# Two layers of graph attention on one core: every engine's steps in another order within the turn, some of them across its border

## What is computed

```python
# layer 0: 6 heads of 64, masked dot-product attention
q, k, v = heads(x @ Wq + bq), heads(x @ Wk + bk), heads(x @ Wv + bv)
probs = softmax(q @ k.T / 8 + where(adj, 0, -9e15))
x = layernorm(x + (probs @ v) @ Wf + bf)
# layer 1: 12 heads of 32, additive attention with a gate
h = x @ W                                  # per head
attn = leaky(tanh(h) @ w_src + (tanh(h) @ w_dst).T, 0.2)
attn = softmax(where(adj, attn, -999))
feat = elu(attn @ h + b)
gate = sigmoid(x @ H_w.T + H_b)
x = layernorm(x + gate * feat + (1 - gate) * x)
```

## Time and profile before

| | |
|---|---|
| median of three runs | 1347.98 us |
| the profiled execution's own time | 1350.65 us |
| its span, from the first to the last instruction | 1348.9 us |
| mean granted clock of TensorE | 0.98 of full speed |
| busy: PE, DVE, POOL, ACT | 1200.5, 1077.4, 1006.0, 990.9 us |
| mean load of the DMA queues | 33 GB/s |
| PE's share of the chain that ended last | 53% |

### The profile page before, as it was taken

How to read it: one execution, slowest core, us unless ns; L and a number is a source line. 1 busy time by engine, 2 the same in 40 slices (tenths; PEclk the granted TensorE clock), 3 DMA queues, 4 the chain that set the end, 5 groups by cost and what they waited for, 6 DMA issues and landing times.

```text
span 1348.9 us, 37937 instructions
## 1 busy us (share of the span) xinstructions
PE 1200.5 (89%) x13193; PEld 1066.4 (79%) x13193; DVE 1077.4 (80%) x2138; ACT 990.9 (73%) x2058; POOL 1006.0 (75%) x941
## 2 busy tenths in 40 slices
PE   4899999999999999999999999999999999999963
PEld 4788788888878888878888887888887888887752
DVE  5478788888888888888888888888888888888864
ACT  4377777777777777777777777777778778777753
POOL 1257877778887777887777788777788777878766
PEclk9799999999999999999999999999999999999976
DMA  3100010111010111101011100011110101110000
GB/s 130 50 27 28 16 39 25 37 37 37 14 37 24 37 37 38 37 14 37 24 37 37 37 19 33 25 36 37 37 37 14 37 24 37 37 37 26 15 13 24
DMA packets 46172, 44.86 MB, mean 33 GB/s; under 512 B 24757, under 2 KB 41146, under 8 KB 46138
## 3 DMA queue, kind: packets, MB, share of 16 engines
q1 hardware_dynamic: 46138, 44.42, 10.1%
HBM read 31.22 MB, written 12.58 MB: 32 GB/s over the span
## 4 chain that ended last, share of the span: by engine, by line
PE 53%; POOL 13%; issue 12%; DVE 10%; ACT 9%; DMA 1%; SPq 0%; DVEq 0%; POOLq 0%; ACTq 0%
PE lin L427 31%; PE tp L600 5%; DVE z L1084 4%; ACT p L785 3%; POOL f L1306 3%; PE zp L528 2%; POOL y L1331 2%; PE tp L565 2%; POOL v_res L1274 2%; PE zp L586 2%; PE fp L612 2%; POOL v_part L1278 2%; PE fp L553 2%; PE zp L590 2%; POOL rstd L1295 1%
## 5 line engine op out<-in xcount | busy, mean ns | idle before, releaser
L1300 POOL TENSOR_TENSOR z<-z,z_max 128x1536 f32<-128x1536 f32 x64 | 176.3, 2755 | 18.0 <-DVE z_max L1091 18.0
L1291 POOL TENSOR_TENSOR rstd<-rstd,half_neg 128x1 f32<-128x1 f32 x64 | 35.2, 549 | 163.3 <-DVE rstd L1071 163.3
L1253 POOL TENSOR_TENSOR prod<-th,w_sd_rows 128x768 f32<-128x768 f32 x64 | 120.1, 1876 | 36.0 <-ACT th L716 36.0
L824 ACT ACTIVATE p1t_hi<-tp 128x512 f16<-128x512 f32 x192 | 110.6, 593 | 37.6 <-PE tp L600 37.6
L1099 DVE SCALAR_TENSOR_TENSOR p1t_lo<-tp,p1t_hi 128x512 f16<-128x512 f32 x192 | 129.4, 688 | 8.0 <-ACT p1t_hi L824 5.0
L612 PE MATMUL fp<-h_part,p1t_hi 128*128 128x33 bf16 x2304 | 115.6, 179 | 4.5 <-DVE p1t_lo L1099 4.4
L612 PEld LDWEIGHTS fp<-h_part,p1t_hi 128*128 128x128 f16 x2304 | 102.5, 97 | 18.4 <-issue 12.7
L600 PE MATMUL tp<-ident,z 128*128 128x128 f32 x768 | 109.5, 280 | 7.4 <-ACT z L819 5.9
L1084 DVE SCALAR_TENSOR_TENSOR z<-zp,z 128x1536 f32<-128x1536 f32 x64 | 111.8, 1748 | 3.2 <-ACT z L794 3.2
L1091 DVE TENSOR_REDUCE z_max<-z 128x12 f32<-128x1536 f32 x64 | 111.3, 1738 | 0.1
L785 ACT ACTIVATE p<-zp,p_shift 128x128 f32<-128x128 f32 x384 | 105.6, 382 | 5.9 <-DVE p_shift L1022 5.9
(11 more groups left out here) (163 smaller groups left out, 4805.3 us busy)
## 6 DMA issues: line engine op xcount, KB each, us to landing
xt_raw<-x_t SPq DMA_DIRECT2D x32, 384.0 KB, 3.6
x_raw<-x SPq DMA_DIRECT2D x32, 384.0 KB, 3.1
out<-out_tile SPq DMA_DIRECT2D x64, 192.0 KB, 1.9
dst_row<-sd_t SPq DMA_DIRECT2D x192, 3.0 KB
adj<-adj SPq DMA_DIRECT2D x64, 32.0 KB, 1.9
z<-Wq SPq DMA_DIRECT2D x1, 576.0 KB, 3.6
z<-Wk SPq DMA_DIRECT2D x1, 576.0 KB, 4.6
p<-Wv SPq DMA_DIRECT2D x1, 576.0 KB, 6.6
```

The costliest lines, as they stand in the source:

```text
L824: act.activation(p1t_hi[:, g, 4 * N * k:4 * N * (k + 1)], tp_bank(f"wt{g}{k}")[:, :], ACT.Copy, scale=PSCALE).then_inc(wt_hi[k][g].sem, 1)
L1253: pool.tensor_tensor(prod[:, g, :].rearrange("p (s d) -> p s d", s=2), th[:, g:g + 1, :].to_broadcast([128, 2, D]), rows["w_sd"][:, :].rea ...
L1300: pool.tensor_tensor(zs, zs, z_max[:, g, :].unsqueeze(2).to_broadcast([128, H1, N]), ALU.subtract)\
```

## The change

The same steps, each engine's in another order; no step is added or removed, and no step itself is touched. Some calls change from `late` to `step` or back, which moves them across the border of a turn. The lists of PSUM users follow:

```diff
-TP_USERS = ("ct1", "wt00", "wt01", "wt02", "x1t0", "wt10", "x1t1", "wt11", "wt12", "pt01", "sdt", "pt00",
-             "pt11", "pt10", "ct0")
+TP_USERS = ("ct0", "ct1", "wt00", "wt01", "wt02", "x1t0", "wt10", "x1t1", "wt11", "wt12", "pt01", "pt00", "sdt", "pt10", "pt11")
-LATE_USERS = ("g1", "z1", "ct1", "pr0", "pr1")
+LATE_USERS = ("ct0", "g1", "z1", "ct1", "pr0", "pr1")
...
+                turn.late(0, context_transposes, 0)
                 turn.late(1, gate_rows, 1)
                 turn.late(1, attention1, 1)
...
-                turn.step(0, context_transposes, 0)
                 turn.step(0, attend0, 1)
...
-                turn.late(1, z_copy, 1)
...
+                turn.step(1, z_copy, 0)
+                turn.step(1, keep_x1, 0)
+                turn.step(0, context_high, 0)
...
+                turn.step(1, z_leak, 0)
+                turn.step(0, context_inverse, 1)
```

More of the change, by code:

```diff
@@ L405, in store @@
                     sp.dma_start(out_d[turn.pair(2), :, g, :], out_tile[:, g, :]).then_inc(stored[g].sem, 16)
-                turn.late(0, load_adj1)
+                turn.late(-1, load_adj0)
                 turn.late(-1, load_x)
+                turn.late(2, store, 0)
+                turn.step(0, load_adj1)
+                turn.step(1, targets_flat)
                 turn.step(-1, load_transposed_x)
-                turn.step(1, targets_flat)
-                turn.step(-1, load_adj0)
-                turn.late(2, store, 0)
                 turn.late(2, store, 1)
@@ L635, in body @@
                 turn.step(2, attend1, 0, 2)
+                turn.step(2, weights1_transposes, 1, 0)
                 turn.step(1, hidden, 0)
-                turn.step(2, weights1_transposes, 1, 0)
                 turn.step(1, x1_transposes, 1)
@@ L1143, in shift_norm1 @@
                         .then_inc(norm1_shift[g].sem, 1)
-                turn.late(0, context_inverse, 1)
-                turn.late(2, variance1, 0)
                 turn.late(0, context_norm, 1)
-                turn.late(1, z_leak, 0)
                 turn.late(0, context_low, 0)
@@ L1331, in mix @@
                     pool.tensor_tensor(y2[:, g, :], f[:, g, :], x1_kept[:, g, :], ALU.add).then_inc(y2_ready[g].sem, 1)
-                turn.late(2, gated_features, 1)
-                turn.late(2, mix, 1)
                 turn.late(-1, next_x_low)
                 turn.late(1, z_subtract, 0)
-                turn.late(1, hidden_part3, 0)
+                turn.late(2, mix, 1)
+                turn.late(1, hidden_part3, 1)
+                turn.step(1, mask1_bias)
                 turn.late(0, deviation0, 0)
                 turn.late(1, z_subtract, 1)
-                turn.late(1, hidden_part3, 1)
                 turn.late(0, deviation0, 1)
-                turn.late(2, deviation1, 0)
                 turn.step(0, value_residue, 0)
@@ L1346, in body @@
                 turn.step(2, features_negative, 0)
+                turn.late(2, deviation1, 0)
                 turn.step(1, source_target_products, 0)
@@ L1349, in body @@
                 turn.step(2, features_difference, 0)
-                turn.step(1, mask1_bias)
+                turn.step(0, value_part3, 0)
+                turn.step(1, hidden_residue, 0)
                 turn.step(2, gated_features, 0)
+                turn.step(0, value_residue, 1)
                 turn.step(2, mix, 0)
-                turn.step(0, value_residue, 1)
-                turn.step(0, value_part3, 0)
                 turn.step(2, features_bias, 1)
                 turn.step(2, features_negative, 1)
+                turn.step(0, value_part3, 1)
                 turn.late(2, deviation1, 1)
-                turn.step(0, value_part3, 1)
-                turn.step(1, hidden_residue, 0)
+                turn.step(1, hidden_residue, 1)
                 turn.step(2, features_difference, 1)
-                turn.step(1, hidden_residue, 1)
+                turn.step(2, gated_features, 1)
+                turn.step(1, hidden_part3, 0)
             turns(pool, passed, body, biases_loaded)
```

87 lines of the change are left out of this document (43 added, 44 removed).

## The result

| | before | after |
|---|---|---|
| median, beside each other on one chip | 1348.32 us (1346.89 to 1348.87) | 1388.49 us (1387.32 to 1389.52) |
| ratio, 95% interval | | 1.0299 [1.0282, 1.0317] |
| span of the profiled execution | 1348.9 us | 1385.6 us |
| mean granted clock of TensorE | 0.98 | 0.946 |

1312 us was forecast; the slower rival was put at 1361 us, and by another mechanism. The turn first, in the timeline of SP of the changed kernel (start and duration in us): the six DMAs of the flat rows, turn by turn.

The account below looks back on a forecast made before the run. The prediction took TensorE's work with holes in the turn's last third as the bound; −1.9 + 0.5 + 0.2 = −1.2 us over 30 turns gave 1312 us. The range was 1278 to 1336 us.

Parts of the forecast that it names:

- the slower rival: The targets' chain comes later because `scores_shift(0)` loses the port: +0.45 us a turn, 1361 us, chance 0.10.
- What bounds the kernel: TensorE's work with holes in the turn's last third; reordering could win some 3 us a turn.
- the two holes: TensorE's stops before `context_transposes(0)`, 1.35 us, and before `attention1(1)`, 0.76 us, laid to steps queued on DVE and ACT.
- Term 1, the end of the turn: `attention1(0)` to the next `attention1(1)`: 3.35 to 3.65 us in place of 5.43, −1.9 us a turn.
- Term 2, the targets' chain: DVE's small steps wait for GpSimd, `source_target_transposes` comes 0.8 us later: +0.5 us a turn.
- the rule in the prediction: On DVE, a step with all inputs in SBUF stands still while a GpSimd step runs; PSUM readers do not.
- Term 3, SP: On SP, the later load of transposed x delays `z_subtract(0)` and TensorE: +0.2 us a turn, 0 to +0.45.
- Term 4: Everything else in the turn keeps its distance from its neighbours within 0.3 us: nothing.
- Parts 2 and 3 don't wait: In the targets' chain they run free of GpSimd: −2.2 us a turn, 1282 us, chance 0.22.
- The gain goes to DMA: On SP, flat rows and transposed x land later: −0.4 us a turn, 1336 us, chance 0.15.
- `scores_shift(0)` loses the port: On DVE it waits for GpSimd's second product, delaying the targets' chain: +0.45 us a turn, 1361 us, chance 0.10.

Follow-up runs that it names:

- Experiment 2: The changed kernel with part 1, residue, part 2 and part 3 as one instruction each over both graphs instead of two: 1313.78 us.
- experiment 3: The kernel before with only `value_part3(0)` and `hidden_residue(0)` moved on GpSimd, right behind `features_difference(0)`: 1387.09 us.
- experiment 1: The changed kernel with GpSimd's `value_part3(0)` and `hidden_residue(0)` back behind `mix(0)`: 1319.62 us.
- experiment 6: The changed kernel with ten unused 512-column matmuls on TensorE ahead of its wait for the targets' chain: 1364.88 us.
- experiment 7: The changed kernel with SP's list as it was before the change: 1382.12 us.
- experiment 8: The changed kernel, chain steps merged, two GpSimd steps behind `mix(0)`: 1307.67 us; then SP's old list: 1300.56; then fewer flat-row DMAs: 1300.44; then `weights0_low(0, 0)` earlier: 1300.37.
- experiment 5: The changed kernel, two variants: GpSimd waits for the targets' chain before `value_part3(0)`, 1378.8 us; TensorE takes `gate_rows(0)` ahead of `source_target_transposes`, 1388.97 us.

## Why the prediction was wrong

**What bounds the kernel, and the two holes: right.** The gain was in the last third of the turn, and both stops named there are gone.

**Term 1, the end of the turn (−1.9 us): right.** From the end of `attention1(0)` (616.60 + 0.81 = 617.41) to `attention1(1)` (620.75) it is 3.34 us; 3.35 to 3.65 was given. That is −2.09 us, and no turn pays for `elu(1)` there: it takes 0.53 us.

**Term 2, the targets' chain (+0.5 us): this step failed, by its size.** The mechanism was right: DVE's small steps stand still behind GpSimd's. The prediction's sum charged one POOL step for each *step* of the chain ("part 1 26.0, residue 27.0, part 2 28.0, part 3 29.1"), when each step is two instructions and each of them lost its turn again. Rows 7 said so and were misread: part 1 at 0.48 us and the residue at 1.07 us for two pieces both lie beside a single POOL step, because GpSimd had a gap behind it; that two pieces together wait once was taken for a rule. The terms as measured:

| | forecast | measured |
|---|---|---|
| start of part 1 | t = 25.7 | 26.3, behind `elu(0)` and the second product |
| part 1 to the end of part 3 | 3.4 us | 5.0 us |
| sdt against before | +0.8 us | +3.0 us |
| rows of `attention1(0)` against before (the term itself) | +0.5 us | +3.3 us, of which the clock 0.8 |

Experiment 2 shows the count (four instructions, 3.2 us), experiment 3 that these two steps suffice, experiment 1 that they are needed. The start of part 1 was taken as unmoved "since `hidden(1)` keeps its place"; `hidden(1)` ends 0.43 us later in the turn. And the rule in the prediction is too wide: not every DVE step with its inputs in SBUF stands still (see the last section).

**What was missing altogether: the clock.** The stretch from sdt to `attention1(0)` grew by 0.26 us, and at the full clock it would have shrunk by 0.5 (experiment 6): 3.0 + 0.26 − 2.09 = +1.17 us a turn as measured, and +0.4 without the fall of the clock. A stop that was priced at its own length cost its length and the speed of what came next. The forecast read the old trace's stops of up to 1.4 us, behind which the clock stays at 1.00, and asked nothing about a longer one.

**Term 3, SP (+0.2 us): nothing in the turn.** ACT's `next_x_high` shows no stop. What SP's order does cost is 6.4 us once, nearly all at the start, by `load_adj0` (experiment 7); filling and draining had been left alone. **Term 4** has no wait of its own in the new trace.

**The sum.** In the two traces the 31 turns from the first sdt to the last one took 37.0 us more, what lies in front of them 1.1 us more, and what lies behind them 1.5 us less: 36.7 us between the spans. The start is only 1.1 us later than before since the new order wins there most of what SP's list loses. Between the medians it is 40.2 us; the rest is that the profiled execution of the kernel before was a slow one of its kind (1350.65 us), and that of the changed kernel the fastest of its (1387.32 us).

**The rivals.** *Parts 2 and 3 don't wait*: wrong for part 2; part 3 ran free only because GpSimd had run out of work (2.46 us idle from 610.26 on). *The gain goes to DMA*: not in this kernel; a wait for the flat rows shows in experiments 6 and 8, and it is worth nothing in the latter. *`scores_shift(0)` loses the port*: it did not, by little. The first product starts at t = 20.87, 0.96 us later than before, and `elu(0)` is held up as that rival had it, but that product's own start moved as well: `scores_shift(0)` starts at 602.94 and the second product at 602.96 us; no `scores_shift` in the whole run takes over 0.17 us. The rival's sign was right and its place wrong, so its sign was luck. With sdt's measured delay in its own sum, +3.0 in place of +0.8, the forecast would have been −1.9 + 2.7 + 0.2 = +1.0 us a turn, 1378 us (of sdt's delay 0.3 us did not reach `attention1(0)` in its sum), without knowing of the clock; the kernel of experiment 6, which has that delay and the full clock, took 1364.88 us.

**The better order exists.** With the chain out of GpSimd's way, the end of the turn keeps the −1.9 us that it promised, sdt still comes 0.6 us later in the turn than before, and the turn is 1.5 us shorter: 1300.56 us.

## What to carry to other kernels

Where two engines share a port, count instructions, not steps or elements: each small instruction on the losing side can cost a whole instruction of the other, so merge the small ones, or leave the other engine a gap beside them. Filling an engine's idle time is free only after asking which engine was running undisturbed in that gap. A stop of TensorE that grows costs its length and, where the granted clock falls behind it as it did here behind stops of 1.8 to 2.7 us, the speed of what comes next. When several edits in a row leave a turn as it is, look for one engine's queue that all of them leave alone.

## What the runs showed of the hardware

- **The port is lost anew with every instruction.** While GpSimd issues back to back, a DVE instruction of 0.13 us (half of the 0.26 us that two take undisturbed) waits for a GpSimd step of 0.9 us, and the next one for another. Where GpSimd has a gap behind its step, however short, the second DVE instruction passes in it as well (0.48 us for two casts beside a gap of 0.08 us, rows 7). The Trainium skill, "SBUF — State Buffer", section "SBUF: two separate sides", has the lock held for one whole instruction by whichever starts first; the rows agree, and add how the turns fall: between two GpSimd instructions that follow without a gap exactly one waiting DVE instruction gets through (each of the five ends 0.03 to 0.04 us behind a GpSimd step), and the next one, right behind it, waits for the whole next step.
- **Not every DVE instruction is held.** The sums (L961, a reduction that reads `prod` in SBUF) lie wholly inside a GpSimd step in 27 of their 64 calls in the changed kernel and take 0.94 us there, as everywhere. So do 128x1 `TENSOR_SCALAR` (L1133, 0.14 us, 31 calls) and the remainders that read PSUM (L1029, 0.54 us, 26 calls). Held were small casts, subtractions of two tiles in SBUF and `elu`, and in other runs `scores_shift(1)` (0.86 us in place of 0.16).
- **The clock falls at a stop of about 2 us, once a turn.** Stops of 1.96, 2.19 and 2.65 us (experiments 5 and 3, and the changed kernel) in practically every turn, and stops of 1.81 us (experiment 5) in 16 turns of 27, with a mean clock of 0.945 to 0.956; stops up to 1.4 us with 0.98. So at 1.8 us the length of the stop alone doesn't decide it. At 1.2 GHz TensorE then ran for some 3 us. Ten matmuls without use in the stop kept it at 2.4 GHz and made the kernel 23.6 us faster.
- **A tie that never cost anything.** `scores_shift(0)` starts 0.01 to 0.02 us before GpSimd's product in the turns read (561.96 and 561.97, 602.94 and 602.96, 643.89 and 643.90), and not one of them waited. In the one turn in which the product starts first, by 0.001 us (1012.56), it did not wait either. What a little more delay would do was not tried.
